# First taps of a depthwise convolution made by GpSimd in a fused four-block network on one core

## The reference

```python
x = x + _L0_conv_ref(_gn(x), v_init, weight, bias)            # whitening by power iteration
x = x + _L1_conv_ref(_gn(x), dw_w, dw_b, ln_g, ln_b, ...)     # deformable convolution
x = x + _L2_conv_ref(_gn(x), w_qkv, window_tokens, ...)       # attention in 7x7 windows
x = x + _L3_conv_ref(_gn(x), weight, bias, mask_weight, ...)  # masked 3x3 convolution
```

```python
x1 = conv_general_dilated(x, dw_w, (1, 1), [(1, 1)] * 2, feature_group_count=C)   # 3x3, depthwise
x1 = transpose(x1, (0, 2, 3, 1)) + dw_b
x1 = gelu(layernorm(x1) * ln_g + ln_b)
offset = x1 @ off_w + off_b
mask = softmax(x1 @ mask_w + mask_b)
```

## Time and profile before

| | us |
|---|---|
| median of 3 runs (lowest, highest) | 9387.29 (9381.67, 9398.54) |
| profiled execution: its own time | 9381.39 |
| profiled execution: span | 9379.5 |
| TensorE matmuls busy | 7921.2 |
| VectorE busy | 7347.3 |
| ScalarE busy | 4158.8 |
| GpSimd busy | 191.4 |

### The profile page before, as it was taken

How to read it: one execution, slowest core, us unless ns; L and a number is a source line. 1 busy time by engine, 2 the same in 40 slices (tenths; PEclk the granted TensorE clock), 3 DMA queues, 4 the chain that set the end, 5 groups by cost and what they waited for, 6 DMA issues and landing times.

```text
span 9379.5 us, 289665 instructions
## 1 busy us (share of the span) xinstructions
PE 7921.2 (84%) x123582; PEld 4467.3 (48%) x123582; DVE 7347.3 (78%) x9217; ACT 4158.8 (44%) x7020; POOL 191.4 (2%) x253
## 2 busy tenths in 40 slices
PE   6457898888988898898889889898988989898897
PEld 6324545454454545444454544445454444545454
DVE  2478887978887887888788788888978888897873
ACT  0034545444454545445454544545454454545432
POOL 0000000000000000000000000000000000000000
PEclk7579999999999999999999999999998999999998
DMA  5000111111021111102011110201111020111101
GB/s 121 0 20 17 50 37 45 42 44 48 26 56 31 51 33 46 46 27 59 28 51 33 47 46 28 60 27 50 33 48 45 29 60 27 49 33 49 45 26 56
DMA packets 231851, 391.62 MB, mean 42 GB/s; under 512 B 26736, under 2 KB 168016, under 8 KB 223312
## 3 DMA queue, kind: packets, MB, share of 16 engines
q1 hardware_dynamic: 230544, 372.67, 14.2%
HBM read 190.38 MB, written 130.55 MB: 34 GB/s over the span
## 4 chain that ended last, share of the span: by engine, by line
PE 60%; DVE 23%; issue 11%; ACT 5%; DVEq 1%; DMA 0%; SPq 0%; POOL 0%; ACTq 0%; POOLq 0%
PE ps L900 11%; PE ps L699 9%; PE ps L765 7%; DVE arena L1737 4%; PE ps L1001 4%; PE ps L798 4%; PE ps L991 3%; PE ps L814 3%; DVE arena L1792 3%; PE ps L773 3%; PE ps L787 2%; PE ps L721 2%; DVE arena L1715 2%; DVE arena L1720 2%; DVE arena L1832 2%
## 5 line engine op out<-in xcount | busy, mean ns | idle before, releaser
L900 PE MATMUL ps<-arena,ident 64*64 64x512 f32 x5600 | 1661.1, 645 | 320.7 <-DVE arena L1737 320.7
L902 PE MATMUL ps<-arena,ident 48*64 48x512 f32 x5600 | 1664.3, 646 | 0.0
L1737 DVE TENSOR_TENSOR arena<-arena 112x2560 f32<-112x2560 f32 x560 | 1577.9, 2819 | 15.7 <-PE ps L902 9.7
L900 PEld LDWEIGHTS ps<-arena,ident 64*64 64x64 f32 x5600 | 463.6, 141 | 1288.8 <-issue 1279.1
L765 PE MATMUL ps<-arena,wqk 128*128 128x400 f32 x2048 | 879.8, 546 | 150.3 <-DVE arena L1841 108.8
L699 PE MATMUL ps<-vp,convw 128*128 128x448 f32 x2016 | 832.3, 551 | 19.2 <-ACT vp L1327 19.2
L814 PE MATMUL ps<-arena 64*64 64x33 f32 x32768 | 635.1, 225 | 118.8 <-issue 76.2
L1243 ACT ACTIVATE arena<-ps 112x864 f32<-112x864 f32 x224 | 199.4, 890 | 1137.4 <-PE ps L721 1132.7
L1720 DVE TENSOR_TENSOR arena<-arena 112x576 f32<-112x576 f32 x896 | 679.3, 758 | 31.0
L1826 DVE COPY arena<-ps 128x400 f32<-128x400 f32 x512 | 292.8, 572 | 520.8 <-PE ps L765 520.4
L1832 DVE TENSOR_REDUCE arena<-ps 128x16 f32<-128x800 f32 x512 | 505.0, 986 | 242.1 <-PE ps L787 238.1
(11 more groups left out here) (301 smaller groups left out, 12773.2 us busy)
## 6 DMA issues: line engine op xcount, KB each, us to landing
windows_out<-arena SPq DMA_DIRECT2D x1024, 100.0 KB
arena<-windows_out SPq DMA_DIRECT2D x224, 256.0 KB, 3.9
arena<-windows_out SPq DMA_DIRECT2D x224, 192.0 KB, 3.3
arena<-in_wqk SPq DMA_DIRECT2D x16, 2048.0 KB, 8.0
arena<-in_x_t SPq DMA_DIRECT2D x16, 1568.0 KB, 11.0
arena<-in_x SPq DMA_DIRECT2D x16, 1568.0 KB, 7.3
arena<-arena SPq DMA_DIRECT2D x32, 784.0 KB
out_x<-xb SPq DMA_DIRECT2D x112, 224.0 KB, 2.0
```

The costliest lines, as they stand in the source:

```text
L900: nc.tensor.matmul(ps[half, 3, :], ident[0:SLOT, 0:SLOT], prod[0:SLOT, ring(c, dy), dx, :], start=(s < 2), stop=(s >= TAPS - 2), skip_grou ...
L902: mm = nc.tensor.matmul(ps[half, 4, :], ident[SLOT:PT, SLOT:], prod[SLOT:PT, ring(c, dy), dx, :], start=(s < 2), stop=(s >= TAPS - 2), ski ...
L1737: V.tensor_tensor(prod[0:PT, ring(c, dy), :, :].rearrange("p k (n e) -> p k n e", e=CG), taps.to_broadcast([PT, SHIFTS, N64, CG]), for_tap ...
```

## The change

GpSimd makes the first two taps of block 1, the first four of block 2 and the first five of block 3 (`DW_FIRST`), as a `tensor_scalar` into the accumulator for the first tap, and for each further one a `tensor_scalar` into a scratch tile `dw_part` and a `tensor_tensor` that adds it to the accumulator. It waits after each instruction for its completion. The last addition of a block raises the new signal `dw_g`, on which VectorE waits ahead of its own first tap of that block. VectorE makes the 25 other taps; `DW_SLOTS` lays them over the same iterations, mostly two in each, and the count of its chain (`DVE_PRE`) is lowered. Block 0 stays with VectorE. `first_taps` stands in GpSimd's program between `zero_windows` and `zero_taps`.

```diff
-DW_SLOTS = (5, 5, 5) + (6, 6, 6) + (7, 7, 7) + (8, 8, 8) + (9, 9, 9) + (10, 10, 10) + (11, 11, 11) + (12, 12, 12) + (13, 13, 13) + (14, 14, 14) + (15, 15, 15) + (16, 16, 16)
+DW_FIRST = (0, 2, 4, 5)
+DW_ORDER = [(b, tap) for b in range(DW_BLOCKS) for tap in range(DW_FIRST[b], P9)]
+DW_SLOTS = (5, 5, 6, 6, 6, 7, 7, 8, 8) + (9, 9, 10, 10, 11, 11, 12) + (12, 13, 13, 14, 14) + (15, 15, 16, 16)
...
-DVE_PRE, DVE_MAIN, DVE_BLK, DVE_END = 6 + 8 * DW_BLOCKS, 98, 69, 61
+DVE_PRE, DVE_MAIN, DVE_BLK, DVE_END = 6 + 8 * DW_BLOCKS - sum(DW_FIRST), 98, 69, 61
...
+        dw_part = arena[:, G_AT + PIX:G_AT + PIX + 2 * CH]
...
+            def first_taps(n):
+                own_dw.turn(n, 2 * sum(DW_FIRST[1:]) - 2 * (DW_BLOCKS - 1))
+                for b in range(1, DW_BLOCKS):
+                    ks = dw_block(b)
+                    rows, size = ROWS * len(ks), CH * len(ks)
+                    acc = x1c[:, ks[0] * CH:ks[0] * CH + size].rearrange("c (h w) -> c h w", w=W)
+                    part = dw_part[:, 0:size].rearrange("c (h w) -> c h w", w=W)
+                    pool.wait_ge(v1_in.sem, v1_in.at(n, min(ks[-1] + 2, CHUNKS)))
+                    alone(pool)
+                    for tap in range(DW_FIRST[b]):
+                        dy, dx = tap // 3, tap % 3
+                        around = vp[:, ROWS * ks[0] + dy:ROWS * ks[0] + dy + rows, dx:dx + W]
+                        own_dw.step(nc.gpsimd.tensor_scalar(part if tap else acc, around, dww[:, tap:tap + 1], None, ALU.mult))
+                        alone(pool)
+                        if tap:
+                            ins = nc.gpsimd.tensor_tensor(acc, acc, part, ALU.add)
+                            if tap == DW_FIRST[b] - 1:
+                                ins.then_inc(dw_g.sem, 1)
+                            else:
+                                own_dw.step(ins)
+                                alone(pool)
+
+            own_dw = Chain(pool, t_dw)
+            first_taps(0)
             zero_taps(None, 0)
             with pool.Fori(0, N - 1) as i:
                 zero_windows(i)
+                first_taps(i + 1)
                 zero_taps(i, i + 1)
+            own_dw.end()
...
-                b, tap = j // P9, j % P9
+                b, tap = DW_ORDER[j]
...
+                if tap == DW_FIRST[b]:
+                    dve.wait_ge(v1_in.sem, v1_in.at(n, min(ks[-1] + 2, CHUNKS)))
+                    if b:
+                        dve.wait_ge(dw_g.sem, dw_g.at(n, b))
                 if tap == 0:
-                    dve.wait_ge(v1_in.sem, v1_in.at(n, min(ks[-1] + 2, CHUNKS)))
```

More of the change, by code:

```diff
@@ L300, in build @@
         d_init, d_a, d_cov, d_pow, d_pre, d_main, d_blk, d_end = (sem(f"dve_own_{k}") for k in range(8))
-        t_main = sem("act_own_main")
+        t_main, t_dw = sem("act_own_main"), sem("pool_own_dw")
         a_xt = [sig("a_xt0", 16), sig("a_xt1", 16)]
@@ L324, in build @@
         cp_col, cp_img = sig("columns_copied", 2 * TY * 16), sig("rows_copied", 2 * 16)
-        dw_d = sig("dw_taps", DW_BLOCKS)
+        dw_d, dw_g = sig("dw_taps", DW_BLOCKS), sig("dw_first_taps", DW_BLOCKS - 1)
         dw_p, dw_s = sig("dw_psum", CHUNKS), sig("dw_sbuf", CHUNKS)
```

## The result

| | before | after |
|---|---|---|
| median of 17 runs, us | 9388.83 | 9414.64 |
| lowest, highest | 9374.79, 9409.78 | 9391.62, 9430.18 |
| profiled execution (span) | 9381.39 (9379.5) | 9406.13 (9404.3) |

The ratio is 1.0022, with a 95% interval of 1.0015 to 1.0030: 14 to 28 us more. Forecast were 9427 us, in a range of 9340 to 9480, slower by about 0.4%. The direction holds, and the size came out at about half to two thirds.

A forecast was written before the change was run, and what follows sets the result against it. Neither VectorE nor TensorE was taken to bound everything; the bound changes by iteration. Profiled 9381.4 us plus 39.5 us (31.5 in 15 passes, 8 in the first image) is 9420.9; the median's 5.9 us more gives 9427, range 9340 to 9480.

The forecast's parts named there:

- The sum: Whole kernel: net +2.1 us a loop pass, +31.5 us in 15, and +8 us in the first image, +39.5 us.
- The removal: VectorE's dropped taps, iterations 5 to 16 and first image: -2.1 us a pass, -9.1 us in the first image.
- The interference: VectorE taps beside GpSimd instructions, iterations 6 to 9: each may wait out the instruction in flight; 4.2 us a pass.
- seven taps of 0.6 us on the path: Three taps in iteration 6, two in 7, place 0 in 8 and 9, each waiting 0.6 us: 4.2 us a pass.
- The waits for GpSimd: VectorE's new waits ahead of blocks 1 to 3, iterations 9, 12 and 15: GpSimd finishes in time, costed at nothing.
- Slack at place 1: Iterations 8 and 9: the tap at place 1, of places 0 to 2, was said to have slack, so not counted.
- B: Rival of the other sign: taps beside GpSimd do not wait at all; -40.6 us, time 9347 us; chance 0.27.
- C: Rival, a draw: taps wait 0.2 to 0.45 us or share a path by turns; 9370 to 9406 us; chance 0.20.
- A: The forecast itself: taps wait out GpSimd's instructions; 9427 us, own range 9406 to 9480; chance 0.48.
- D: Rival: GpSimd needs over 8.9 us per instruction of block 1, so VectorE waits in iteration 9; 9500 us; chance 0.05.
- The signs: Profile: taps about 0.6 us longer or late; maxima of iterations 5, 7 about 1 us nearer, 9, 10, 12, 13 unchanged.
- The last sign: Taps and other instructions beside GpSimd: the prediction is wrong if instructions with one SBUF input also wait; no size given.

The follow-up runs named there:

- e1_no_gpsimd: The changed kernel with GpSimd's taps left out: VectorE makes its 25 taps in the changed slots and waits for nobody; 9351.9 us, 0.9964 of the kernel before.
- e3_mults: The changed kernel with GpSimd's 11 multiplications alone, its 8 additions left out; 9362.2 us, 0.9977 of the kernel before.
- e11_memsets: The changed kernel with memsets for GpSimd's work, three per multiplication and two per addition; 9360.2 us, 0.9970 of the kernel before.
- e2_beside: The kernel before, all 36 taps on VectorE, with GpSimd running the same 19 instructions beside them into an unread scratch tile; 9486.5 us, ratio 1.0112.
- e12_later_gates: The changed kernel with additions released by VectorE signals (blocks 2 and 3 later), later tap places from iteration 9, image 0 on VectorE alone; 9352.4 us, ratio 0.9970.
- e8_gated: The changed kernel with each of GpSimd's 8 additions also waiting for a signal VectorE raises after an iteration's last tap; 9418.1 us, 1.0022 of the kernel before.

## Why the prediction was right, and where its terms were off

**The sum.** The mechanism held: GpSimd's reads hold taps up, and this costs more than the removal gives. The size is smaller. Forecast were +2.1 us a pass and +8 in image 0; the table has +0.6 (95.3 - 94.7), and image 0 +8.6. That is 17 us, within the measured 14 to 28. The loop's +0.6 is the small difference of two terms that were both off, and that it kept its sign has some luck in it.

**The removal.** Forecast -2.1 us a pass, iteration by iteration -1.2, 0, -1.0, +0.24, -0.2, -0.1, -0.3, 0, 0, +0.46, 0, 0. e1_no_gpsimd against before: -1.27, -0.14, -0.78, +0.17, -0.17, -0.05, -0.09, -0.11, 0, +0.34, -0.42, -0.09, in sum -2.6. Reading each iteration from the end of the scores and the start of the next maximum was sound; of 9.07 us of VectorE's work a pass gives back less than a third. e1's 34 us in all agree with the forecast 40.6 within the interval (23 to 45). In image 0 7.6 us came off, not all 9.1.

**The interference.** Forecast 4.2 us a pass and 17 us in image 0, 80 us; shown by e1 against the kernel after are 3.2 us a pass (95.3 - 92.1) and 16 in image 0, 64 us by the traces and 54 (41 to 67) by the times. The term is "seven taps of 0.6 us on the path". Three taps of a usual pass wait instead, 1.23, 0.44 and 1.36 us. The number was too large because the term took every GpSimd instruction to hold a tap up for the rest of its time, and the wait too small because GpSimd's instructions are longer. Two errors met. GpSimd's instructions are much longer than I took: a multiplication of 896 elements 2.52 us undisturbed where I took 1.2 (above even my upper end of 1.6), an addition 2.08 us for 1.6. And the multiplications, 65% of GpSimd's time (412 of 637 us), hold a tap up in their first 0.8 us only (e3_mults). By iteration, forecast 1.8, 1.2, 0.6, 0.6 in 6 to 9; shown 1.26, 0.01, 0.57, 1.08. The rule that I weighed there (the Trainium skill, SBUF — State Buffer, section Who interferes with whom) agrees with the additions and, for what only writes, with e11_memsets; it is too broad for the multiplications, beside which a tap that starts later runs in 1.14 to 1.18 us. The estimate of 1.97 us for an addition (the Trainium skill, GPSIMD Engine Reference, section Performance versus the Vector engine) agrees with the measured 2.08.

**The waits for GpSimd.** At nothing inside the loop, as forecast: GpSimd's work of a pass begins at 1448.1 and ends at 1490.5 us in the pass cited, in time for iterations 9, 12 and 15. In image 0 two waits of 2.0 and 7.1 us came in, which the forecast did not name. Its +8 was a discount on GpSimd and VectorE taking turns; that 8.6 came of other parts is luck.

**Slack at place 1.** I gave place 1 slack in iterations 8 and 9. In iteration 8 it has none, as the pass cited shows, where the tap of 2.25 us stands there (9.45 us instead of 8.35): the second half of the input projection waits for the copy L1858 behind it. The row of TensorE in the kernel after, behind the tap of 2.25 us:

```profile
1472.39 1.12 PE L736 MATMUL ps<-inw,arena 128*112 128x128 f32 x8 [0.95 <-DVE arena L1858]
```

**The rivals.** B (no waiting, 9347) is what e1 and e11 are; the kernel would be there if GpSimd's work did not read. C (up to 9406) is missed by 9 us only, and the +0.6 us of a loop pass lies in C's own -0.7 to +1.0: by the time alone A and C are hardly parted. What parts them is the mechanism: the taps do not all wait a little, two or three of a pass wait over 0.4 us and the others hardly at all. D falls: GpSimd is slower than I took it, but 2.5 us are far from 8.9.

**The signs.** Taps beyond 1142 ns and the maxima of iterations 5 and 7 nearer together came as named. The maximum of iteration 9 was to be unchanged and came 0.9 us later; that contradicted the forecast's own 0.6 us there. The last sign, an instruction with one SBUF input that waits too, cannot be ruled out: in e2_beside 4 of the 64 first taps of a block, which have one such input, took 0.35 to 0.75 us more than their usual 0.68 or 0.44, one of them with no GpSimd instruction beside it. It was not followed up.

**Left open.** Iterations 17 to 29 took 97.3 us in the kernel after and 95.9 before, but 94.9 to 97.2 in the other traces without any order; the second stage took 315.0 and 316.0, 315.5 to 317.5 in the others. I count no part of either to the change, though each is larger than the +0.6 us of the stretch with the taps; where the terms of the sum rest on the traces, this is their uncertainty.

## What to carry to other kernels

An engine that takes work over at a quarter of the speed can help, but count first what it does to the instructions beside it: here some 54 us of waiting ate more than the 34 us gained. Before moving elementwise work, find the iterations where the relieved engine really ends last, and put the remaining work at the place that no other engine waits for, iteration by iteration; moving two taps within the iteration brought 28 us and cost nothing. A release that a queue raises behind an instruction can come before this instruction starts (e12_later_gates); a wait in front of it should help, which was not tried. And before one pass of a loop is read as the loop, compare it with the others: the one cited here was of a kind that 3 of 15 were.

## What the runs showed of the hardware

- A VectorE tap (`scalar_tensor_tensor`, two SBUF inputs) that finds a GpSimd addition (`tensor_tensor`, two SBUF inputs) in flight ends 0.95 us after the addition: 2.37, 2.25 and 2.64 us for 1.14. The other way round an addition that finds a tap in flight grows too (2.99 instead of 2.08 us in e8_gated).
- Beside a GpSimd multiplication by a column (one SBUF tensor) it depends on the start. In the loop, a tap that starts in the first 0.8 us of the multiplication ends 1.95 us after the multiplication's start (1.74 us for a start 0.21 us into it, in e3_mults); one that starts later (1.15 us and more) keeps its 1.14 to 1.18 us, and the multiplication grows from 2.52 to 2.9 or 3.4 us. Beside memsets no tap changes (1143 ns in e11_memsets).
- GpSimd's multiplication by a column is slower than its addition of two tensors: 2.52 against 2.08 us at 896 elements, 1.40 against 1.13 at 448, which is 2.5 and 2.1 ns an element; VectorE's multiply-and-add takes 1.04 for both at once.
- The granted clock of TensorE fell from 1.00 to 0.50 (1.2 GHz) for 3.4 us in iteration 7 of three of the 15 passes and not in the other twelve; four matmuls (L794) took 3.03 us instead of 1.61 in it.
